# Second attention: full key tiles' weights all split into high and low parts, the ring of split parts cut from five slots to four

## What is computed

```python
q = rmsnorm((hidden_states @ Wq).reshape(B, Sq, H, D), gq)            # B=4, Sq=256, H=16, D=128
k = rmsnorm((encoder_hidden_states @ Wk).reshape(B, Skv, H, D), gk)   # Skv=1601, cdim=128
v = (encoder_hidden_states @ Wv).reshape(B, Skv, H, D)
scores = jnp.einsum('bqhd,bkhd->bhqk', q, k) * scale
attn = jax.nn.softmax(scores, axis=-1)
out = jnp.einsum('bhqk,bkhd->bqhd', attn, v).reshape(B, Sq, H * D)
x = x + jnp.tanh(g_xattn[1]) * (out @ Wo)
```

## Time and profile before

| | us |
|---|---|
| median of three runs | 1975.44 |
| lowest, highest | 1975.04, 1980.54 |
| the profiled execution's own time | 1977.05 |
| its span, first to last instruction | 1974.9 |

### The profile page before, as it was taken

The page is one execution under the profiler, slowest core; times in us unless marked ns, Lnnn a source line. Parts: engine busy times, 40 slices in busy tenths (PEclk is TensorE's granted clock), DMA queues, the critical chain, the costliest instruction groups (busy, mean ns, idle before and its releaser), DMA issues. The chain is left out here.

```text
span 1974.9 us, 31470 instructions
## 1 busy us (share of the span) xinstructions
PE 1829.2 (93%) x9085; PEld 1342.2 (68%) x9087; DVE 1366.6 (69%) x2268; ACT 1162.3 (59%) x1943; POOL 336.6 (17%) x298
## 2 busy tenths in 40 slices
PE   5789898949999889999899998999989998999998
PEld 3444444547888667776677766777667776788887
DVE  8565656245666678877778787878778786666665
ACT  2577666813333567776677767777667774333222
POOL 3010101023444300001000010000100002444442
PEclk9899999969999999999999999999999997999999
DMA  3413223155443200001000010000000001455553
GB/s 93 105 49 73 70 53 77 29 170 127 112 113 85 67 1 0 0 0 34 0 0 0 0 34 0 0 0 0 1 1 0 0 0 38 88 112 112 114 114 82
DMA packets 110127, 96.58 MB, mean 49 GB/s; under 512 B 72836, under 2 KB 94472, under 8 KB 109416
## 3 DMA queue, kind: packets, MB, share of 16 engines
q1 hardware_dynamic: 110056, 95.67, 19.7%
HBM read 73.73 MB, written 1.44 MB: 38 GB/s over the span
## 5 line engine op out<-in xcount | busy, mean ns | idle before, releaser
L902 ACT ACTIVATE s_p<-ps,s_g,s_rk 128x256 f32<-128x256 f32 (+1 forms) x832 | 412.3, 559 | 126.4 <-PE ps L1129 91.5
L1129 PE MATMUL ps<-s_qq,s_ctxT 128*128 (+2 forms) x1248 | 389.6, 425 | 18.4 <-ACT s_p L902 15.7
L423 PE MATMUL ps<-s_xT,s_wgus 128*128 128x512 f32 x1440 | 350.5, 393 | 3.0 <-DVE s_hw L1643 2.6
L423 PEld LDWEIGHTS ps<-s_xT,s_wgus 128*128 128x128 f32 x1440 | 272.2, 189 | 62.1 <-DVE s_hw L1643 3.4
L1129 PEld LDWEIGHTS ps<-s_qq,s_ctxT 128*128 128x128 f32 (+1 forms) x1248 | 231.7, 187 | 106.7 <-issue 47.2
L1129 PE MATMUL ps<-s_ps,s_ctx 128*128 128x512 f32 x960 | 276.5, 398 | 0.1
L817 ACT ACTIVATE s_p<-ps,s_bsm 128x1024 f32<-128x1024 f32 x208 | 219.1, 1111 | 96.1 <-PE ps L1010 85.0
L1763 DVE TENSOR_TENSOR s_dsum<-s_dsum,s_p 128x512 f32<-128x512 f32 (+1 forms) x352 | 242.2, 688 | 30.4 <-ACT s_p L902 19.6
L1772 DVE TENSOR_TENSOR s_ps<-s_p,s_ps 128x512 fp32r<-128x512 f32 x320 | 220.1, 688 | 13.2 <-ACT s_ps L908 9.8
L1129 PEld LDWEIGHTS ps<-s_ps,s_ctx 128*128 128x128 f32 x960 | 182.2, 190 | 46.7 <-DVE s_ps L1772 1.8
L1645 DVE TENSOR_TENSOR s_hs<-s_hw,s_hs 128x512 fp32r<-128x512 f32 x120 | 138.7, 1156 | 82.3 <-ACT s_hs L346 82.3
(11 more groups left out here) (253 smaller groups left out, 2128.5 us busy)
## 6 DMA issues: line engine op xcount, KB each, us to landing
s_wB<-w1s SPq DMA_DIRECT2D x64, 256.0 KB, 4.0
s_kT<-s_kst SPq DMA_DIRECT2D x96, 128.0 KB, 2.3
s_kT<-s_kst SPq DMA_DIRECT2D x96, 80.0 KB, 2.1
s_wB<-w0s SPq DMA_DIRECT2D x16, 384.0 KB, 3.8
s_wB<-w0s SPq DMA_DIRECT2D x16, 256.0 KB, 4.0
s_wgu<-in_L_ffn_Wg_dram SPq DMA_DIRECT2D x64, 64.0 KB, 3.0
s_wgu<-in_L_ffn_Wu_dram SPq DMA_DIRECT2D x64, 64.0 KB, 2.7
s_wd<-in_L_ffn_Wd_dram SPq DMA_DIRECT2D x64, 64.0 KB, 2.7
```

The costliest lines, as they stand in the source:

```text
L423: ins = nc.tensor.matmul(ps[:, 4 + g, :], wgus[:, slot, w, g, k, :], xT[:, x_, k, n], start=c == 0, stop=c == len(ops) - 1)
L902: ins = nc.scalar.activation(p1[0:r, SLOT1[t], j, :], ps[0:r, BANK1[t], j * SQ:(j + 1) * SQ], ACT.Exp, bias=g1[0:r, 3:4], scale=rk_col(t, ...
L1129: ins = nc.tensor.matmul(out, lhs(x_), rhs(y_), start=first and n == 0, stop=last and n == 2)
```

## The change

Tiles 3 and 7 become split tiles. So all twelve full tiles' weights are split and go through three matmuls, and only the short tile stays whole. VectorE casts the high parts of tiles 1 and 6 (before: 2, 6 and 10), ScalarE those of the other ten (before: seven). The ring of split parts has four slots in place of five; the memory that it gives up goes to the filler behind it. ScalarE's copy of the context of tiles 3 and 7 goes, and `ctx_kept` counts two steps a batch instead of three.

```diff
-SPLIT1 = (0, 1, 2, 4, 5, 6, 8, 9, 10, 11)
-HI_DVE = (2, 6, 10)
+SPLIT1 = tuple(range(KT - 1))
+HI_DVE = (1, 6)
 HI_ACT = tuple(t for t in SPLIT1 if t not in HI_DVE)
-WHOLE1 = (3, 7, 12)
-RING1 = 5
+WHOLE1 = (12,)
+RING1 = 4
...
-                    sp.wait_ge(s.ctx_kept, 3 * b)
+                    sp.wait_ge(s.ctx_kept, 2 * b)
...
-                    pool.wait_ge(s.ctx_kept, 3 * (tt // TB) + 1)
+                    pool.wait_ge(s.ctx_kept, 2 * (tt // TB) + 1)
...
-                nc.scalar.copy(ctxw[:, 0:2, :], st[:, 3:8:4, :]).then_inc(s.ctx_kept, 1)
-                nc.scalar.copy(ctxw[0:ROWS1[-1], 2, :], st[0:ROWS1[-1], KT - 1, :]).then_inc(s.ctx_kept, 1)
+                nc.scalar.copy(ctxw[0:ROWS1[-1], 0, :], st[0:ROWS1[-1], KT - 1, :]).then_inc(s.ctx_kept, 1)
...
-                pe.wait_ge(s.ctx_kept, 3 * (b + 1))
+                pe.wait_ge(s.ctx_kept, 2 * (b + 1))
```

## The result

| | before | changed |
|---|---|---|
| median us | 1980.28 (6 runs, 1975.04 to 1982.56) | 1966.61 (6 runs, 1961.72 to 1968.49) |
| ratio to before, 95% interval | | 0.9934, 0.9915 to 0.9953 |
| the profiled execution, own time / span | 1977.05 / 1974.9 | 1965.27 / 1963.4 |

The change makes the kernel faster. The first comparison has 13.7 us between its medians, the most of the three; its six executions of before have a mean of 1979.3. The forecast was 3.4 us.

What follows compares the result with a forecast made beforehand. TensorE's own stream was taken to bound the steady pairs. A gain of 7.0 us less 3.6 lost in last pairs gave 3.4 us faster: median 1975.44 - 3.4 = 1972.0 us, range 1965 to 1978.

Steps and rivals of the forecast that it cites:

- within 0.3%: Whole kernel: outcome within about 0.3% (5.9 us) of before, not to be told from no change; chance 0.57.
- rival A: TensorE's products run at 0.69 us in all places, a pair gains 0.47; 9.6 us faster, 1965.8; chance 0.20.
- TensorE, tiles 3 and 7: Steady pairs: 22 places of three matmuls at 0.70 us, a gain of 0.25 a pair, 7.0 us over 28.
- the four first pairs: Each batch's first pair: same 0.25 us gain put in; clock spread of 1.85 us kept for the range.
- ScalarE's chain and the last pairs: Batch ends: three more ScalarE casts a pair bring tile 11's low part 0.90 us later; 3.6 us lost over four.
- The cover in the 28 other pairs: Pairs with a pair behind them: tile 11's later low part stays hidden, with about 0.55 us to spare.
- Rival C: ScalarE becomes the pace, tile 11's low part over 0.55 us late; 8.1 us slower, 1983.5; chance 0.07.
- ScalarE's pair-end cover: Before the next pair's tile 3: ScalarE keeps 2.1 us of its earlier 3.27 us wait for scores.
- VectorE: Each pair: 0.8 us more work out of 2.84 idle; tile 3's low part in time by 0.28 us.
- rival D: Tile 3's low part is late, a pair gains 0.1 us; 0.8 us slower, 1976.2; chance 0.12.
- Rival E: VectorE or ScalarE is the true bound, each pair grows by 0.8 us; 25.6 slower, 2001; chance 0.03.
- The ring, the cast of tile 1, the copy into `ctxw`: Ring of four (1.6 us cover), VectorE casting tile 1 instead of 2, dropped 0.40 us ScalarE copy: each predicted nothing.

Runs made afterwards that it cites:

- The first comparison: Changed kernel against the kernel before, six runs each: 1966.61 against 1980.28 us, ratio 0.9934; two further comparisons of the same kernels gave 0.9950 and 0.9955.
- One cast more: Changed kernel with tile 6's cast on ScalarE too, so VectorE casts tile 1 alone: one run of 1974.92 us.
- the added copies: Changed kernel with four unneeded copies of 100 columns a pair on VectorE ahead of `oT1`: one run of 1967.32 us.
- The repetitions: The changed kernel with no edit, compared twice more with the kernel before: ratios 0.9950 and 0.9955.

## Why the prediction was right or wrong

The changed kernel came out at 1966.61, inside the range (1965 to 1978), faster by more than the 0.3% that I could tell from no change; I had given "within 0.3%" the larger chance. The sign was right, the size was not: 9.0 us against 3.4. The median lies inside the range because the range was drawn to hold most of rival A, and about a third of A's additional gain came true (below). By the pairs alone the median would be 1975.44 - 5.9 = 1969.5; that it came out 3 us lower is in no term of the forecast, and so near to the lower end partly chance.

**TensorE, tiles 3 and 7** (0.25 us a pair, 7.0 in all). The term was mis-sized. It measured 21.445 - 21.127 = 0.32, times 28 is 8.9 us (with the four first pairs put in at the same value, as in the forecast). The forecast's stream (0.70 in every place, pair of 21.20) came true in 15 of 24 pairs, each 0.25 shorter as said. The other nine are rival A's up to the 65-key product (0.69, pair of 21.02), 0.43 shorter. I had weighed them as one or the other. The step under it, that the 0.69 stretch goes with the whole tile ahead of it, held: tile 3 alone is worth 0.105. That such a stretch can also start at a pair's head with no whole tile near was left to rival A, with a chance of 0.20; the term rested on "products that follow a pair's start with no whole tile between run at 0.70", and that sentence was wrong for the changed kernel.

**ScalarE's chain and the last pairs** (4 x 0.90 = 3.6 lost). Right in mechanism, and nearly in size. The cast of tile 11 was put at 13.43 behind tile 3's exponentials and stands at 13.43. Its low part follows 0.66 behind (896.16 to 896.82), not 0.73, so it comes 0.83 later. The exponentials of tile 3 start 0.08 earlier behind the product with `m1` (2.86 against 889.67 - 886.73 = 2.94 in the same pair before), so 0.75 is left, and the last pairs grew by 0.74 to 0.78: 3.0 us. Both signs that I had named are there, waits of 0.54 and 1.09 and a stretch of 4.10 us. One cast more moved a last pair by 0.71, and one less in the chain gave it back.

**The cover in the 28 other pairs** (0.55 us). In a steady pair of the changed kernel:

```profile
832.76 0.62 ACT L907 CAST s_ps<-s_p 128x512 fp32r<-128x512 f32 x1
...
833.42 0.69 DVE L1771 TENSOR_TENSOR s_ps<-s_p,s_ps 128x512 fp32r<-128x512 f32 x1
...
834.84 0.65 PEld L1128 LDWEIGHTS ps<-s_ps,s_ctx 128*128 128x128 f32 x3
```

The load could have come 0.74 behind the low part's start, at 834.16, and stood at 834.84: a cover of 0.68 after the change, somewhat more than the 0.55 laid out, because the low part followed its cast sooner. In the nine fast pairs, where TensorE comes earlier, it is 0.50. Rival C (ScalarE becomes the pace) would have needed it used up. A chain 0.71 longer did use it up, and cost the steady pair 0.04.

**ScalarE's pair-end cover** (2.1 us of 3.27). The wait for tile 3 is 58.6 / 28 = 2.09 us in the mean, against 91.5 / 29 = 3.16 before. Right.

**VectorE** (0.8 us out of 2.84 idle; tile 3's low part in time by 0.28). The wait ahead of `oT1` went from 2.84 to between 1.54 and 1.74. It shrank by more than 0.8 because the pair got shorter as well. No wait for a low part shows in any steady pair, so rival D didn't occur. Rival E is refuted by the added copies. By the Trainium skill (Perfetto Trace Analysis, Identifying the Most-Contended Engine) TensorE is judged by its arithmetic against the peak and by the busy share of its weight loads, and the engine with the highest occupancy is the one to relieve. Of the shares that the rows give, VectorE's is the highest in the pair shown: 18.23 of 21.01 us, against 17.70 of ScalarE and 16.79 of the weight loads. The runs go against it: 0.67 us more on VectorE came with a shorter pair, and 0.57 on top with an unchanged one.

**The ring, the cast of tile 1, the copy into `ctxw`** (nothing). The ring of four on the old kernel, and the split with the old ring and the old casts, show nothing for the first two. Where casts lie does matter within the chain from tile 3 to 11: moved to tiles 4 and 7 they undo most of the last pairs' loss (20.31 to 19.65, against 19.56 before). The copy was not tried by itself.

**The sum.** By the pairs it is 8.9 - 3.0 = 5.9 us, not 3.4. The attention as a whole went from 991.5, 990.6 and 990.5 (before twice, and with the ring of four) to 986.2, 981.6 and 983.5, 7.1 in the mean. So 1 us lies in first pairs and between batches. The timings give 9.0, with an interval of 7.3 to 10.5, and 8.3 at the same granted clock. What is left outside the attention, 1 to 2 us, is no more than the uncertainty of either number; parts that the change doesn't touch differ by more from one execution to the next. The mean clocks of the two kernels differ by 0.0004, worth some 0.5 us, so a change in how long the clock is low isn't what carries the gain. Whether memory places add a little stays open.

## What to carry to other kernels

Take the durations from the starts of a pipelined engine's rows, and before adding work to another engine lay out its chain from the last point that the bound engine sets: that gave the start of tile 11's cast to 0.01 us and its low part to 0.07. Then ask where in the program this chain is not hidden (here the one pair in eight with no scores between its values), and put the casts that can be moved inside that chain, not ahead of it. When an effect is under 1% of the time, read it in the repeating unit, whose mean over 24 pairs here repeats to 0.03 us for the same program, and don't explain the span of single executions, which differ by over 10 us. Where each execution has its mean granted clock beside it, compare at the same clock: here that halves the uncertainty of the difference.

## What the runs showed of the hardware

- A stream of three-matmul products at the full clock has two paces, 0.70 us a product and 0.69 (0.68 and 0.70 in turn), with the same instructions. In the changed kernel's first profile it kept one of them from a pair's start up to the 65-key product, behind which all pairs run at 0.70, and neighbouring pairs differed. The repetitions also have a few pairs of 21.08 us, with an even 0.69 up to there. With a full whole tile left in the pair, none of 24 pairs has the faster stream from its start. What picks the pace was not found. By the Trainium skill (TensorE: Matmul & The Clock Gate, Back-to-back issue gap) the spacing in a stream of loads and matmuls is set by both, and it is given as some 131 ns at 512 columns, or about 216 ns for a matmul by itself. By an estimate from these figures three would take 0.39 or 0.65 us. The rows don't agree: they are at 0.69 to 0.70, 0.23 us a matmul, at the full clock in every kernel here.
- A whole tile's call of plain fp32 costs 0.86 us in the stream (1.56 with the product behind it at 0.70), against 0.70 for the split tile's three matmuls: 23% more.
- The length of a stretch at TensorE's 1.2 GHz, in the same place of an unchanged stage, was 20.5 us in one execution and 6.8 and 3.4 us in another of the same program, worth 2.7 us of the span: a quarter of the 10.3 us by which they differ.
- Over 61 executions of the kernel before and 24 of the changed one, the time falls by 1.1 us for each 0.001 of mean granted clock, with some 1.5 us of scatter left. 0.001 is 4 us at 1.2 GHz in place of 2.4, so the whole kernel loses about a quarter of such a stretch too.
